# First batch of three attentions scored in fp32 from row groups of eight, before the split bf16 operands of the other batches are in place

## The reference, cut to what matters

```python
q = (xn @ Wq.T + bq) * 8 ** -0.5        # heads of 8 channels
k = ctx @ Wk.T + bk
v = ctx @ Wv.T + bv
scores = einsum("bhqd,bhkd->bhqk", q, k) + adj      # adj: 256 x 256
scores = where(mask, scores, -inf)                  # per batch; the second and third by key padding
x = x + tanh(g) * (softmax(scores) @ v @ Wo.T + bo)
```

## Time and profile before

| what | value |
|---|---|
| median of 3 runs | 862.73 us (861.38 to 862.84) |
| the profiled execution, its own time | 862.37 us |
| its span, first to last instruction | 860.4 us |
| PE busy | 702.3 us, 82% |
| DVE busy | 573.1 us, 67% |
| ACT busy | 488.9 us, 57% |
| POOL busy | 166.6 us, 19% |
| mean granted PE clock | 0.898 |
| first score of the three attentions | 41.57, 179.03, 470.31 us |

### The profile page before, as it was taken

How to read it: one execution, slowest core, us unless ns; L and a number is a source line. 1 busy time by engine, 2 the same in 40 slices (tenths; PEclk the granted TensorE clock), 3 DMA queues, 4 the chain that set the end, 5 groups by cost and what they waited for, 6 DMA issues and landing times. The chain is left out here.

```text
span 860.4 us, 14382 instructions
## 1 busy us (share of the span) xinstructions
PE 702.3 (82%) x4728; PEld 396.0 (46%) x4728; DVE 573.1 (67%) x1765; ACT 488.9 (57%) x1323; POOL 166.6 (19%) x135
## 2 busy tenths in 40 slices
PE   4589994559997878999744899949999999869978
PEld 2266663336665323333222667635336666644322
DVE  3699995869996358667865999855316666436553
ACT  2288881259883568598812988812666556413201
POOL 8622000420000045536655000020000000000000
PEclk8689997769999768998885999979999999969999
DMA  8895004060000000000009200000000000000000
GB/s 310 169 319 177 2 7 69 23 126 2 2 2 2 0 1 0 1 0 1 1 0 180 41 2 2 2 26 0 1 0 1 1 2 2 1 1 1 0 1 24
DMA packets 22056, 32.26 MB, mean 38 GB/s; under 512 B 1760, under 2 KB 15712, under 8 KB 21216
## 3 DMA queue, kind: packets, MB, share of 16 engines
q1 hardware_dynamic: 21984, 31.36, 14.4%
HBM read 21.39 MB, written 9.96 MB: 36 GB/s over the span
## 5 line engine op out<-in xcount | busy, mean ns | idle before, releaser
L816 ACT ACTIVATE RING<-RING,NMX 128x256 f32<-128x256 f32 x384 | 190.7, 500 | 56.2 <-DVE NMX L1637 55.8
L1637 DVE CUSTOM_DVE_ANT_0 RING<-bank,ADJM 128x256 f32<-128x256 f32 x384 | 143.4, 413 | 23.5 <-DMA scratch<-RING 22.5
L1158 PE MATMUL bank<-W,RING 128*128 128x128 f32 x768 | 120.5, 282 | 15.6 <-ACT RING L828 13.9
L541 POOL TENSOR_TENSOR small<-small 128x8 f32<-128x8 f32 (+2 forms) x13 | 17.7, 1365 | 463.1 <-DVE small L1528 463.1
L1158 PEld LDWEIGHTS bank<-W,RING 128*128 128x128 f32 x768 | 91.7, 145 | 27.9 <-ACT RING L816 23.2
L1138 PE MATMUL bank<-ARENA 128*128 128x256 bf16 x384 | 77.8, 290 | 30.7 <-DMA ARENA<-scratch 25.7
L1649 DVE COPY RING<-bank 128x512 f32<-128x512 f32 x144 | 98.6, 686 | 1.2 <-PE bank L1158 0.8
L816 ACT ACTIVATION_READ_ACCUMULATOR RING<-RING,NMX 128x1 f32 x384 | 72.8, 190 | 0.0
L997 PE MATMUL bank<-XT,W 128*128 128x512 f32 (+2 forms) x118 | 62.2, 668 | 6.6 <-ACT XT L712 5.3
L728 ACT ACTIVATE RING<-bank,NMX 128x512 f32<-128x512 f32 x64 | 43.4, 683 | 41.8 <-PE bank L1062 21.2
L1280 PE MATMUL bank<-ARENA,W 64*128 64x512 f32 x180 | 62.3, 710 | 3.6 <-DVE ARENA L1830 2.3
(11 more groups left out here) (253 smaller groups left out, 1307.3 us busy)
## 6 DMA issues: line engine op xcount, KB each, us to landing
scratch<-ARENA SPq DMA_DIRECT2D x18, 256.0 KB, 3.2
ARENA<-scratch SPq DMA_DIRECT2D x6, 768.0 KB, 10.6
W<-in_weights SPq DMA_DIRECT2D x1, 2564.0 KB, 21.2
scratch<-RING SPq DMA_DIRECT2D x36, 64.0 KB, 3.0
ARENA<-scratch SPq DMA_DIRECT2D x12, 192.0 KB, 3.8
scratch<-RING SPq DMA_DIRECT2D x18, 128.0 KB, 2.9
ARENA<-scratch SPq DMA_DIRECT2D x6, 384.0 KB, 6.6
W<-in_weights SPq DMA_DIRECT2D x2, 1024.0 KB, 13.7
```

Source lines behind the costliest of these rows:

```text
L816: nc.scalar.activation(P_OF(n)[:, q * S:(q + 1) * S], S_OF(n)[:, q, :], ACT.Exp, bias=NMX[:, 2 * t + q:2 * t + q + 1], scale=-1.0, accum_o ...
L1158: mm = nc.tensor.transpose(bk[:, o:o + P], P_OF(n)[:, i:i + P], ident)
L1637: nc.vector.tensor_tensor_reduce(out=S_OF(n)[:, q, :], in0=SBANK(n)[:, q * S:(q + 1) * S], in1=ADJM[:, b, q, :], scale=-1.0, scalar=BIG, o ...
```

## The change

The first batch of each of the three attentions no longer needs the split operands. Its keys and queries are multiplied out with 32-column weights, four heads at a time, so that the eight channels of head j stand on partitions 32j to 32j + 7 (K32 and Q32, fp32, in the quarter of KS and QS that the first batch would have had). Each of its scores is two fp32 matmuls over eight rows. Biases in that layout (BKQ) are made once by 16 small matmuls.

The split, written and read operands hold the other 768 tokens, the queries in two pieces (`LATER`). Their transposes, products and, in the first attention, the values, and the output row of the first and third, are issued from within the loop, in steps 1, 3, 4 and 5, through a new ring `rh` of banks 6 and 4. All splitting is done by POOL. The mask terms are cut: DVE finishes those of batch 0 of the first attention (`first_masks`), and does the others' first part in step 6 (`other_masks`). POOL makes masks of batches 0 and 1 of the second and third attention earlier. Keys of the second and third attention are made after the first. The clearing leaves out the first batch's part, and the third attention's clearing is cut in two, most of it after its normalization. The third attention's first keys and its values are started amid the end of the experts' part. SP loads CT and W ahead of X, masks by batch, and the second weights after the first attention's transfers.

```diff
+LATER = [(S, 2 * S), (2 * S, 4 * S)]
+KEY_CUTS = [(S, S + 512), (S + 512, TOK)]
+        Q32 = ARENA[:, 0:8192].rearrange("p (h t) -> p h t", h=H16)
+        K32 = ARENA[:, 8192:12288].rearrange("p (j t) -> p j t", j=H16 // 2)
         @block.sync
+            sp.dma_start(CT[:, :], ctxT_in).then_inc(s_ldc, 16)
+            sp.dma_start(W[:, 0:EDGES[1]], w_in[:, 0:EDGES[1]]).then_inc(s_ld[0], 16)
             sp.dma_start(X[:, :, :], x_in).then_inc(s_ldx, 16)
...
             def queries(a):
-                for k in range(len(PIECES) + 1):
+                for k, (t0, t1) in enumerate(LATER):
+                    write(3 + a, QP, ((0, 3, 5), (1, 4), (2,)), t0, t1, s_qp, 3 * (len(LATER) * a + k), s_qw[k])
+                    read(3 + a, lambda e: QS[64 * e:64 * e + 48, e::2, :], t0, t1, s_qw[k], 96 * (a + 1), s_qs[k])
...
             write_keys(1)
-            write_keys(2)
             sp.wait_ge(s_s, UNITS)
             read_keys(1)
             queries(1)
+            write_keys(2)
             sp.wait_ge(s_zero, 2)
         @block.gpsimd
+            def three_parts(src, parts, done, n, first=True, second=True):
+                if first:
+                    nc.gpsimd.tensor_copy(parts[:, 0, :], src).then_inc(done, 1)
+                    pool.wait_ge(done, n + 1)
+                    link(nc.gpsimd.tensor_tensor(src, src, parts[:, 0, :], ALU.subtract))
+                if second:
+                    nc.gpsimd.tensor_copy(parts[:, 1, :], src).then_inc(done, 1)
+                    pool.wait_ge(done, n + 2)
+                    nc.gpsimd.tensor_tensor(parts[:, 2, :], src, parts[:, 1, :], ALU.subtract).then_inc(done, 1)
...
+            clear_queries(0, H16)
+            clear_keys()
+            clear_pads()
             pool.wait_ge(s_set, 1)
             roots()
+            key_parts(0)
+            query_parts(0)
             pool.wait_ge(s_set, 2)
-            masks(0)
-            for a in (1, 2):
-                for step in range(4):
-                    key_parts(a, step)
+            masks(0, 1, B)
+            masks(1, 0, 2)
             root()
+            key_parts(1, second=False)
             pool.wait_ge(s_am, 2)
             nc.gpsimd.partition_all_reduce(AMAXR, AMAX, P, bass.bass_isa.ReduceOp.max).then_inc(s_amr, 1)
+            key_parts(1, first=False)
             roots()
-            masks(1)
+            query_parts(1)
+            masks(1, 2, B)
+            key_parts(2)
             root()
...
+            pool.wait_ge(s_xnext, 2 * NC)
+            clear_queries(10, H16)
             pool.wait_ge(s_int, 2 * NC)
-            clear_queries()
-            clear_rest()
             roots()
-            masks(2)
+            pool.wait_ge(s_xn, 5 * NT)
+            clear_keys()
+            clear_queries(0, 10)
+            clear_pads()
+            query_parts(2)
+            masks(2, 2, B)
         @block.scalar
+                        if t == 3:
+                            later_queries(a)
+                        if t == 4 and a == 0:
+                            values(0, NC, rh, s_he)
+                        if t == 4 and a != 1:
+                            out_row(rh, s_he)
+                        if t == 5:
+                            first_queries(a, 2, NG, rh, s_he)
         @block.tensor
+            def heads(out, name, g, rhs):
+                for j in range(HG):
+                    f = DH * (HG * g + j)
+                    mm = nc.tensor.matmul(out[PAD * j:PAD * j + PAD, :], w(name, f, f + PAD), rhs, start=True,
+                                          stop=True)
+                return mm
...
+                    turn(XN, 0, TPB)
+                    pe.wait_ge(s_ea, ra.n)
+                    first_queries(a, 0, 2, rk, s_fk)
...
+                    if t < UNITS and b == 0:
+                        if j == 0 and g < 2:
+                            pe.wait_ge(s_ek, rk.n - 1 + g)
+                        elif j == 0:
+                            pe.wait_ge(s_he, HE_AT[a] + HE_N[a] - 3 + g)
                         if n >= 3:
                             pe.wait_ge(s_max, 2 * n - 4)
+                        r = slice(PAD * j, PAD * j + DH)
+                        for q in range(2):
+                            mm = nc.tensor.matmul(
+                                SBANK(n)[:, q * S:(q + 1) * S].rearrange("p (k c) -> p k c", k=2),
+                                Q32[r, 2 * g + q, 0:P], K32[r, 2 * g:2 * g + 2, 0:P], start=True, stop=True)
+                        mm.then_inc(s_s, 1)
+                    if t == 1:
+                        for t0, t1 in LATER:
+                            turn(XN, t0 // P, t1 // P, rh, s_hf)
+                    if t == 3:
+                        later_queries(a)
+                    if t == 4 and a == 0:
+                        values(0, 0, NC, rh, s_hf)
+                    if t == 4 and a != 1:
+                        out_row(a, rh, s_hf)
+                    if t == 5:
+                        first_queries(a, 2, NG, rh, s_hf)
+                    if t < UNITS and b > 0:
+                        pe.wait_ge(s_max, 2 * n - 4)
                         bk = SBANK(n)
+                        if t == 16:
+                            pe.wait_ge(s_ks, 32 * (a + 1))
                         if t % 16 == 0:
-                            pe.wait_ge(s_qs[min(b, 2)], 32 * (a + 1))
+                            pe.wait_ge(s_qs[min(b - 1, 1)], 32 * (a + 1))
...
+            biases()
             attention(0)
+            pe.wait_ge(s_ld[1], 16)
+            keys(1)
             turn(XN)
+            keys(2)
+            first_keys(1, 0, NG)
+            out_row(1, ra, s_fa)
...
             for c in range(NC):
+                if c == 1:
+                    r6.drain(pe, (2, 3, 6, 7))
+                    first_keys(2, 0, 2)
+                    values(2, 0, 1, ra, s_fa)
                 pe.wait_ge(s_int, NC + c + 1)
...
+            values(2, 1, NC, ra, s_fa)
+            first_keys(2, 2, NG)
         @block.vector
                     layernorm(X, XN, cuts=((0, TPB), (TPB, NT)))
                     if a == 0:
-                        mask_terms()
-                    for k, (t0, t1) in enumerate(PIECES):
...
-                        nc.vector.tensor_copy(QP[:, 0, t0:t1], q).then_inc(s_qp, 1)
...
-                    for k in range(len(PIECES)):
-                        dve.wait_ge(s_qw[k], 96 * (a + 1))
+                        first_masks()
...
+                        if a == 0 and t == 6:
+                            other_masks()
```

More of the change, by code:

```diff
@@ new lines, in first_queries, with later_queries, values @@
+            def first_queries(a, g0, g1, ring, full):
+                for g in range(g0, g1):
+                    heads(ring.fill(pe)[:, 0:S], f"wq{a}", g, XT[:, 0:S]).then_inc(full, 1)
+            def later_queries(a):
+                for k, (t0, t1) in enumerate(LATER):
+                    pe.wait_ge(s_he, HE_AT[a] + 1 + k)
+                    product(rh, [(w(f"wq{a}"), XT[:, t0:t1])], s_hf)
+            def values(a, c0, c1, ring, full):
+                for c in range(c0, c1):
+                    bk = ring.fill(pe)
+                    for i in range(4):
+                        t = 4 * c + i
+                        mm = nc.tensor.matmul(bk[:, i * D:(i + 1) * D], CT[:, t * P:(t + 1) * P], w(f"wv{a}"),
+                                              start=True, stop=True)
+                    mm.then_inc(full, 1)
@@ L1019, in latents, with out_row @@
+            def out_row(a, ring, full):
+                product(ring, [(col(f"bv{a}", g), w(f"wo{a}", g * P, (g + 1) * P)) for g in range(NG)]
+                        + [(w("ones", 0, 1, rows=1), w(f"bo{a}", rows=1))], full)
             def latents():
```

301 lines of the change are left out of this document (161 added, 140 removed).

## The result

The changed kernel took 885.07 us (median of 4, 880.05 to 887.63), beside 862.06 for the kernel before on the same chip: a ratio of 1.0263, 95% interval 1.0213 to 1.0313. It is slower by 2.6%; the forecast was 849.3, in a range of 832 to 862. The profiled execution took 886.11 with a span of 884.3, 23.9 more than before. Some executions of a kernel take over 1.5% longer than its fastest; the ratios leave these out, and the medians count them.

A forecast was written before the change was run, and what follows sets the result against it. Attention loops run near three engines' limits, with nobody full ahead of them. Loops starting 60.7 us earlier, mostly spent on dearer scores and moved matmuls, gain 15.9; less 2.5 for quantizing, 13.4: 862.7 to 849.3 us, range 832 to 862.

The forecast's parts named there:

- Sixteen units on TensorE after the change: Each attention's first 16 units: scores 17.8, transposes 5.6, value products 2.3, spreading 0.6; 26.3 us at full clock.
- 3 us of low clock in the third attention: Third attention's first units run at the clock of 0.50 found before its loop, adding 3 us.
- The forecast sums: First score to batch 1's first score, with moved work and stalls: 36.1, 30.5 and 35.2 us in the three attentions.
- full from the fourth microsecond or so of each loop: Expected sign in the profile after: granted clock at 1.00 from about the fourth microsecond of each attention's loop.
- Rival 3: Eight-row scores leave the clock low for each attention's first 16 units: +79 us, or +26 for a third, 875; chance 0.07.
- First scores: Start of the three attention loops, at 17.2, 165.2 and 447.8 us, 60.7 us earlier in all.
- A score: One unit's two eight-row fp32 matmuls on TensorE, not overlapping: 0.93 + 0.18 = 1.11 us.
- rival 2: Weight loads of the eight-row scores don't hide: 48 x 0.84 = 40 us more, 889; chance 0.10.
- Rival 1: Score pair or its neighbours overlap, so ScalarE's pace sets the loop: some 18 us less, 831; chance 0.10.
- Transfers at unit 16: Query parts through scratch are ready 11 to 14 us before batch 1's first score; priced at nothing.
- Masks in step 6: First attention: VectorE makes three batches' masks in about 4.4 us; 2 us of it remain as TensorE's wait.
- The quantizing stretch: POOL's key parts beside VectorE's normalizing and grid operations cost 2.5 us, between 0 and 4.8.

The follow-up runs named there:

- the run with zeros: Changed kernel with single first-batch scores over the 32 rows of a row group, the queries' other 24 rows zero: 841.62 us, 0.9804 of the kernel before.
- the run over 128 rows: Changed kernel with the first batch's scores over all 128 rows instead of eight (output differs): 832.7 us, one execution.
- The pairs: Changed kernel with scores of heads j and j + 1 issued together on two row groups, eight rows each: 839.2 us, 0.9734 of the kernel before.
- full-height fillers: Changed kernel with useless full-height bf16 matmuls ahead of each eight-row score: one of identity 912.8 us, one of dense data 909.3, four dense 933.1.
- the run with POOL's order alone: Changed kernel with all POOL's key parts of the second attention after the roots of its normalization: 901.2 us, one execution.
- 32 rows of data: Changed kernel with single first-batch scores over 32 rows, 24 holding neighbouring heads' values (output differs): 851.74 us, one execution.

## Why the prediction was wrong

**The step that failed** is the clock that the 16 units were priced at: "Sixteen units on TensorE after the change ... 26.3 us at full clock", with 3 us of low clock in the third attention alone. The runs showed low clock in all three, worth 43.8 us: 13.4, 16.8 and 13.6, against ways with the same instructions over 32 rows. The forecast sums were 36.1, 30.5 and 35.2 us; measured 50.3, 45.2 and 43.3. The rest of the sums was about right: without the 3 us they are 98.8 us, and the same stream took 36.9, 28.4 and 29.7, together 95.0, at a clock of 0.95, 1.00 and 1.00. With the clock up in most of the ways the change is worth what was forecast or more: 841.62 us in the run with zeros, forecast 849.3.

The kernel before could have warned of the 3 us. In each of its attentions the clock was low behind the first score too, without any score over eight rows, in the first for some 9 us, from 41.57 to the step at 50.85, where the transposes go from 0.85 us to 0.44:

```profile
49.70 1.06 PE L1158 MATMUL bank<-W,RING 128*128 128x128 f32 x4
50.55 0.46 PE L1138 MATMUL bank<-ARENA 128*128 128x256 bf16 x2
50.85 0.60 PE L1158 MATMUL bank<-W,RING 128*128 128x128 f32 x4
51.29 0.38 PE L1138 MATMUL bank<-ARENA 128*128 128x256 bf16 x2
```

Its ways had 0.76, 0.79 and 0.81. The clock that the prediction expected, full from the fourth microsecond or so of each loop, is in no row of it and did not come.

**The rival.** Rival 3 had the mechanism, the low clock with eight-row scores, and a chance of 0.07. It was held down by "clock 1.00 in a stretch in which the transposes are the longest part". That row was right and beside the point: it has full-height transposes and 128-row value products, and none of the rows that the prediction cites has matmuls of so few rows for a large part of the time. The Trainium skill (TensorE: Matmul & The Clock Gate, Part 4) says that transposes do not bring the clock up. That does not explain it either, and the trace disagrees: the run over 128 rows has the same transposes and a clock of 0.93 to 1.00. Its size, 26 us for a third of the time at half clock, was over half of the 43.8 us measured.

**Point by point.**
- First scores, forecast 17.2, 165.2, 447.8: measured 15.08, 173.66, 469.30. The last two are late because what stands ahead of them was; from the last normalization's first statistics (159.38 before, 167.81 after) to the first score the second took 5.85 us, forecast 5.8.
- A score: forecast 1.11 us, measured 1.06 at full clock. The dearer price of rival 2, exposed weight loads, is out. Rival 1, that the two matmuls of a unit overlap, is out as well; the overlap is there between units of different row groups, as the earlier trace rows said. The pairs have it, and so have the first two units of the changed kernel (at 15.08, eight records in 1.07 us until the next instruction).
- Transfers at unit 16: hidden, as forecast.
- Masks in step 6: VectorE works on them from 35.81 to 40.42 in the trace after, 4.6 us, forecast 4.4. TensorE, at full clock there, had no wait for VectorE behind it, so of the 2 us forecast nothing came; the pairs, in which TensorE is further ahead, wait 3.17 us.
- The quantizing stretch: forecast 2.5, in bounds of 0 to 4.8; measured 4.4. The hold of VectorE's operations was named, and it is 3.8 of the 4.4. That the reduction starts 5.7 us after POOL's last operation before it was not seen, although it is in the trace of the kernel before too: the root ends at 143.06 and the reduction starts at 148.80.

**What stays open.** Why the clock goes with the rows at all, why full-height fillers do not raise it, and how it depends on the number of rows between 8 and 128. Single executions of like kernels differ a lot here: the third way is the same code in the run with POOL's order alone, but had a clock of 0.50 there, and 0.65 in the changed kernel; the first way had 0.69 over 32 rows of data and 0.95 over 32 rows with zeros. In the first way the fastest runs in pairs stay below full clock (0.82 to 0.90), for a reason not found.

## What to carry to other kernels

In this kernel a matmul that addresses few rows was dear twice: it took as long as one over 128 rows (1.06 us a score against 0.96), and with much of it in the stream everything else on TensorE ran at the low clock too. Try to address the whole row group, with zeros in one operand where the sum must not change, and to issue matmuls of different row groups together. Work that is moved away from one stretch meets other work in the next: look there for the same hold. When a plan moves work onto the engine that sets the pace, price it at both clock levels, and read the clock of the window, not only the busy share.

## What the runs showed of the hardware

- TensorE can be busy without a gap and still have its clock at half: 30.10 of 30.10 us busy with a granted clock of 0.50 in the changed kernel, right behind 5.90 of 5.90 at 1.00.
- 24 rows of zeros more per score, at no other change, brought 885 to 841.6 us.
- Two scores of 128x256 fp32 on two row groups take 1.06 us together, one alone 1.06.
- POOL's reduction over partitions started 5.63 to 6.64 us after the end of POOL's operation ahead of it in every trace here. In the changed kernel a cast of 0.89 us followed at once, and then 6.79 us passed before POOL's next subtraction.
- VectorE's operations last longer beside POOL's: eight normalizing ones 4.08 us in place of 2.14, six of them 5.67 in place of 1.63.
